# Expert tiles: the tokens' transposes move from TensorE to 32x32 block transposes on VectorE

## The chip, the cores and the metric

The kernel runs on one core of one Trainium2 chip. Times are device microseconds of one execution. The kernel before takes 1641.98 us, the median of 3 runs (1639.44 to 1642.45).

## The reference

Two layers work on x of 4 x 512 tokens with 512 features; each adds an attention part and a feed-forward part to x, and each part reads the layer-normed x. Layer 0 has a score attention against a context and a Hadamard-rotated, quantised feed-forward network. Layer 1 has an attention with 32 heads and then the routed mixture of experts, which is what the change touches:

```python
logits = jnp.einsum('td,de->te', x, gate_w)
top_logits, top_idx = jax.lax.top_k(logits, K)          # K = 2 of E = 8 experts
top_w = jax.nn.softmax(top_logits, axis=-1)
cw = jnp.zeros((T, E)).at[jnp.arange(T)[:, None], top_idx].add(top_w)
for e in range(E):
    h = jax.nn.silu(x @ w0[e]) * (x @ w1[e])            # 512 -> 1024
    out = out + cw[:, e:e + 1] * (h @ wo[e])            # 1024 -> 512
```

T is 2048 tokens, and everything is fp32.

## The kernel before

All stages before the experts keep their code and aren't described here. The last of them sorts the tokens: each token's normed row of 512 values, with its weight for the chosen expert in column 512, is written to `sorted_x` in HBM twice, once for each of its two experts, at a place where the tokens of one expert follow each other. The experts then work on tiles of 128 sorted rows. There are always 39 tiles (`MTILES`), also where the experts have fewer; a small table, `tile_plan`, says for each tile where its rows lie, which expert's weights it takes and where its result goes. Each engine reads its entries of the plan into registers with a load (TENSOR_LOAD in the order of instructions).

The order of the work is written out by hand, one program for each engine, held together by semaphores. `tile_loop` runs the steps 0, 1 and 2, then a hardware loop of two steps a turn, then the last two steps. A step i has these parts:

- ScalarE's DMA queue loads the rows of tile i + 2 (`load`, L1539), 128 rows of 528 values.
- TensorE multiplies tile i by the gate and the up weights (`products`, L2976 to L2978): two halves of 512 inner columns, 24 products each. An fp32 value is kept as two fp32r parts, so that a product of a 128-row chunk is three instructions: first part by first, first by second, second by first.
- TensorE transposes the rows of tile i + 1 into bank 4 of PSUM (`transpose_x`, L2954): four transposes of 128x128.
- TensorE multiplies the inner values of tile i - 1 by the down weights (`down`), 24 products, and then transposes the inner values of tile i (L2999), 8 transposes.
- ScalarE takes the Silu of each half (L1555), copies the transposed tokens as their first part (`x_first`, L1547) and the transposed inner values as theirs (L1560), and issues the store of the result (`store`, L1543).
- VectorE multiplies Silu and up (L2236), makes the second parts (`x_second`, L2256, and L2246), scales the result by the row weight (`move_y`, L2263) and copies the row weight out of the loaded tile (`row_weight`, L2252).
- GpSimd splits the weights of the coming experts into their parts (L1075, L1076). It starts on an expert's down weights when the last down block of the expert before is done. SP loads the weights.

Semaphores that the text speaks of: `e_ld` (a tile's rows are loaded), `e_xtr` (transposed), `e_xh` and `e_xl` (first and second part made), `e_gu` (a half of gate and up is done), `e_xw` (row weight), `e_y` (result scaled), `e_hl` (second part of the inner values). Ahead of the first tile TensorE runs `unread` products (L2860), whose results nobody reads, and waits for the sorted rows; VectorE works out the places of the results (`result_slots`, L2272 to L2279).

## Time and profile before

| | us |
|---|---|
| median of 3 runs | 1641.98 |
| profiled execution | 1643.14 |
| its span | 1641.3 |
| TensorE busy in the span | 1565.4 (95%) |
| VectorE busy | 938.9 (57%) |
| ScalarE busy | 717.1 (44%) |
| GpSimd busy | 702.1 (43%) |
| mean granted TensorE clock | 0.985 of full |
| first expert product | 928.31 into the span |

The expert loop is the stretch from 928 us to the end. In the rows below, PE is TensorE, DVE VectorE, ACT ScalarE, POOL GpSimd; SPq and ACTq are DMA issues of SP and ScalarE. A row in order of time has the start (us from the span's start), the duration (us), engine, line and operation, output <- inputs, the shape, and in brackets the idle time of the engine ahead of it and what ended it. Matmuls overlap: two starts tell more than one duration. "issue" is time in which an engine waited for nothing that the profile shows. A row of the busy time by stretches has the stretch, its length, then the busy time (and number of instructions) of PE, the weight loads of PE, DVE, ACT and POOL, the granted clock of TensorE as a share of 2.4 GHz, the DMA engines' busy share and GB/s. A row of a line's instructions has their count, the least, median and greatest duration in ns, and the first and last start. A row of the page's costliest groups has the busy time and mean ns after the first bar, and the idle time before with what ended it after the second.

### The profile page before, as it was taken

The page shows a single profiled execution, that of the slowest core. Times are in us where ns is not written, and L with a number is a line of the kernel's source. Part 1 is how long each engine was busy: PE and PEld are TensorE (multiplying, and loading weights), DVE is VectorE, ACT ScalarE, POOL GpSimd, SP SyncE. Part 2 cuts the span into 40 slices and gives each one's busy share as a digit, 9 for nine tenths or more (in the row PEclk, how much of TensorE's full clock was granted, in tenths as well). Part 3 has the DMA queues.
Part 4 walks back from the last instruction along what each step waited for, and adds up shares of the span by engine and source line. Part 5 has one row for each costly group of instructions (what it writes and reads, how often), then busy time and mean ns, then how long its engine had stood idle before and what let it go on. Part 6 is the DMA issues. An engine that isn't in the chain of part 4 may idle for free.

```text
span 1641.3 us, 24692 instructions
## 1 busy us (share of the span) xinstructions
PE 1565.4 (95%) x8277; PEld 1046.3 (64%) x8278; DVE 938.9 (57%) x1540; ACT 717.1 (44%) x1166; POOL 702.1 (43%) x479
## 2 busy tenths in 40 slices
PE   6879999999999999999998799999999999999998
PEld 4565757575753333434333788888888888888886
DVE  6898979797888898988884622222222222222221
ACT  5885646464537777777676211111111111111111
POOL 2224352534513125353464756651781270930074
PEclk9889999999999999999999999999999999999999
DMA  9189800000331445353431642323421323510088
GB/s 355 51 306 386 323 1 1 1 1 1 101 80 49 134 125 155 91 146 102 146 104 61 211 155 95 132 77 137 179 77 34 133 77 128 180 39 26 32 142 211
DMA packets 90945, 196.18 MB, mean 120 GB/s; under 512 B 7153, under 2 KB 9074, under 8 KB 90226
## 3 DMA queue, kind: packets, MB, share of 16 engines
q1 hardware_dynamic: 71746, 156.68, 28.5%
q0 software_dynamic: 7168, 17.04, 4.6%
q10 hardware_dynamic: 11952, 21.43, 3.9%
q8 instruction: 46, 0.75, 0.2%
q14 instruction: 33, 0.27, 0.1%
HBM read 113.28 MB, written 81.32 MB: 119 GB/s over the span
## 4 chain that ended last, share of the span: by engine, by line
PE 78%; DVE 13%; ACT 3%; issue 3%; POOL 2%; DMA 1%; another core or an unknown queue 0%; SPq 0%; DVEq 0%; POOLq 0%; ACTq 0%
PE psum L2976 13%; PE psum L2978 13%; PE psum L2977 13%; PE psum L2619 7%; PE psum L2830 6%; PE psum L2819 5%; PE psum L2634 5%; DVE neg_max L2094 4%; PE psum L2793 3%; PE psum L2664 3%; PE psum L2999 2%; DMA x_tiles<-in_x 1%; PE psum L2954 1%; DVE ternary_rows L1697 1%; PE psum L2809 1%
## 5 line engine op out<-in xcount | busy, mean ns | idle before, releaser
L2094 DVE TENSOR_REDUCE neg_max<-psum 128x2 f32<-128x1024 f32 x248 | 291.9, 1220 | 44.1 <-PE psum L2793 42.0
L1450 ACT ACTIVATE probabilities<-psum 128x512 f32<-128x512 f32 x512 | 270.3, 603 | 82.2 <-PE psum L2819 78.1
L2236 DVE TENSOR_TENSOR expert_inner<-psum,expert_inner 128x512 f32<-128x512 f32 x78 | 53.9, 692 | 382.6 <-ACT expert_inner L1555 377.5
L2976 PE MATMUL psum<-expert_weight_parts,sorted_tokens_t_first 128*128 x624 | 249.7, 400 | 4.9 <-issue 3.1
L2978 PE MATMUL psum<-expert_weight_parts,sorted_tokens_t_second 128*128 x624 | 246.3, 395 | 0.0
L2977 PE MATMUL psum<-expert_weight_parts,sorted_tokens_t_first 128*128 x624 | 246.2, 395 | 0.0
L1555 ACT ACTIVATE expert_inner<-psum 128x512 f32<-128x512 f32 x78 | 46.7, 599 | 390.2 <-PE psum L2978 390.2
L2819 PE MATMUL psum<-query_rows,key_rows 50*128 50x512 f32 x512 | 181.4, 445 | 5.1 <-ACT probabilities L1450 1.7
L2793 PE MATMUL psum<-key_rows,query_rows 48*128 48x512 f32 x496 | 173.0, 480 | 6.0 <-DVE neg_max L2094 3.3
L2830 PE MATMUL psum<-probabilities,value_and_one 128*32 128x512 f32 x1024 | 139.8, 619 | 1.5 <-ACT probabilities L1450 0.9
L2976 PEld LDWEIGHTS psum<-expert_weight_parts,sorted_tokens_t_first 128*128 128x128 f32 x624 | 117.3, 188 | 32.4 <-issue 5.9
L2819 PEld LDWEIGHTS psum<-query_rows,key_rows 50*128 50x128 f32 x512 | 78.3, 187 | 90.0 <-issue 37.7
L2978 PEld LDWEIGHTS psum<-expert_weight_parts,sorted_tokens_t_second 128*128 128x128 f32 x624 | 117.4, 188 | 27.3
L2977 PEld LDWEIGHTS psum<-expert_weight_parts,sorted_tokens_t_first 128*128 128x128 f32 x624 | 117.4, 188 | 26.2
L1075 POOL CAST expert_weight_parts<-wo_of_expert 128x2048 fp32r<-128x2048 f32 x16 | 30.4, 1897 | 241.5 <-PE psum L2978 241.5
L1560 ACT ACTIVATE expert_inner_t_first<-psum 128x512 fp32r<-128x512 f32 x78 | 42.6, 596 | 202.0 <-PE psum L2999 202.0
L2976 PE MATMUL psum<-expert_weight_parts,expert_inner_t_first 128*128 128x512 f32 x312 | 125.9, 403 | 1.6 <-DVE expert_inner_t_second L2246 1.6
L2978 PE MATMUL psum<-expert_weight_parts,expert_inner_t_second 128*128 128x512 f32 x312 | 122.2, 392 | 0.0
L2977 PE MATMUL psum<-expert_weight_parts,expert_inner_t_first 128*128 128x512 f32 x312 | 122.1, 391 | 0.0
L2263 DVE TENSOR_SCALAR expert_out<-psum,row_weight 128x512 f32<-128x512 f32 x39 | 29.3, 750 | 161.0 <-PE psum L2978 156.9
L866 POOL TENSOR_TENSOR inner_half_rotated_t<-inner_t 128x512 f32<-128x512 f32 x56 | 75.4, 1367 | 80.0 <-DVE inner_t L1935 79.7
L1028 POOL TENSOR_TENSOR x_tiles<-x_tiles,attended_normed 128x256 f32<-128x256 f32 x31 | 22.7, 733 | 202.2 <-DVE attended_normed L2141 202.2
(317 smaller groups left out, 2966.0 us busy)
## 6 DMA issues: line engine op xcount, KB each, us to landing
sorted_x<-zero_rows SPq DMA_DIRECT2D x9, 3960.0 KB, 30.5
w_of_odd_expert<-in_L_ffn_w SPq DMA_DIRECT2D x8, 2048.0 KB
wo_of_expert<-in_L_ffn_wo SPq DMA_DIRECT2D x7, 2048.0 KB, 8.5
query_rows<-query_rows_of_units SPq DMA_DIRECT2D x64, 192.0 KB, 3.5
w_of_even_expert<-in_L_ffn_w SPq DMA_DIRECT2D x6, 2048.0 KB, 10.7
sorted_tokens<-sorted_x ACTq DMA_DIRECT2D x39, 264.0 KB, 2.7
sorted_y<-expert_out ACTq DMA_DIRECT2D x39, 256.0 KB, 2.1
query_rows_of_units<-dims_first SPq DMA_DIRECT2D x32, 256.0 KB
```

Of the source, the lines that this page charges most:

```text
L866: nc.gpsimd.tensor_tensor(Z[:, chunk_of(r, h) * SEQ:(chunk_of(r, h) + 1) * SEQ], y[0], y[1], op).then_inc(b_half, 1)
L1450: nc.scalar.activation(prob[t % 2][:, i * SEQ:(i + 1) * SEQ], ring(("score", n)), ACT.Exp, scale=HD ** -0.5).then_inc(c_e, 1)
L2094: nc.vector.tensor_reduce(of_pair[:, p, st, :], ring(("max", (m, i))).rearrange("p (h n) -> p h n", h=2), AX.X, ALU.max, negate=True).then ...
L2236: nc.vector.tensor_tensor(h, bank[2 * half + 1], h, ALU.mult).then_inc(e_h, 1)
L2619: last = nc.tensor.matmul(bank[4 + 2 * w + h], wgu_t[w][:, k * FF + f * P:k * FF + (f + 1) * P], q_t[:, k * SEQ:(k + 1) * SEQ], start=(k = ...
L2634: last = nc.tensor.matmul(bank[4 + g], y[:, at:at + P], had[:, k * D:(k + 1) * D], start=(k + part == 0), stop=(k + part == DC))
L2793: done = nc.tensor.matmul(ring(job)[:, h * SEQ:(h + 1) * SEQ], q_r[m % 4][rows, p * SEQ + st * P:p * SEQ + (st + 1) * P], k_r[m % 4][rows, ...
L2819: nc.tensor.matmul(ring(("score", n)), k_r[u % 4][rows, t * P:(t + 1) * P], q_r[u % 4][rows, p * SEQ:(p + 1) * SEQ], start=True, stop=True ...
L2830: last = nc.tensor.matmul(bank[7][32 * h:32 * h + 32, :], v_u[u % KVH][:, t * 32:(t + 1) * 32], prob[t % 2][:, h * SEQ:(h + 1) * SEQ], sta ...
L2976: nc.tensor.matmul(out_bank, hi[:, cols], w_r[:, bass.ds(w_at, 512)], start=start, stop=False)
L2977: nc.tensor.matmul(out_bank, hi[:, cols], w_r[:, bass.ds(w_at + BLOCK, 512)], start=False, stop=False)
L2978: return nc.tensor.matmul(out_bank, lo[:, cols], w_r[:, bass.ds(w_at, 512)], start=False, stop=stop)
```

## The change

TensorE's four token transposes go. In their place VectorE transposes the tile as 32x32 blocks in one instruction (`x_transposed`), from SBUF into bank 4, between the two halves' products of the step. A block transpose alone doesn't bring features across groups of 32 partitions, so the load does: tile i is loaded by four DMAs (`load`, a = 0 to 3), each of which places the 128 features a*128 to a*128 + 127 of all 128 rows on 32 partitions. The features then stand in bank 4 in another order, and the host lays out the rows of `w0` and `w1` in that order (`laid_out`), outside the kernel. The row weight is no longer part of the tile; it has its own load of 16 columns, straight into `row_w` (`load_row_weight`), behind the store of a step. The inner values are transposed on TensorE as before.

```diff
-        x_in = [small.tile(f"sorted_tokens{i}", [P, WIDE]) for i in range(2)]
+        x_in = [small.tile(f"sorted_tokens{i}", [P, D]) for i in range(2)]
...
-        row_w = [small.tile(f"row_weight{i}", [P, 1]) for i in range(2)]
+        row_w = [small.tile(f"row_weight{i}", [P, WIDE - D]) for i in range(2)]
...
-            sp.wait_ge(e_ld[1], 16)
+            sp.wait_ge(e_ld[1], 64)
...
                 def load(i, parity):
-                    act.wait_ge(e_xtr, i + 1)
                     if not (static(i) and i < 2):
-                        act.wait_ge(e_xw, i - 1)
-                    nc.scalar.dma_start(x_in[parity][:], sorted_x[bass.ds(row_of(i), P), :]).then_inc(e_ld[parity], 16)
+                        act.wait_ge(e_xtr, i - 1)
+                    rows = sorted_x[bass.ds(row_of(i), P), 0:D]
+                    for a in range(4):
+                        nc.scalar.dma_start(x_in[parity][32 * a:32 * a + 32].rearrange("r (b c) -> r b c", c=P),
+                                            rows[:, a * P:(a + 1) * P].rearrange("(b r) c -> r b c", r=32)).then_inc(e_ld[parity], 16)
+
+                def load_row_weight(i, parity):
+                    if not static(i) or i > 0:
+                        act.wait_ge(e_xw, 16 * i)
+                    if not static(i) or i > 1:
+                        act.wait_ge(e_y, i)
+                    nc.scalar.dma_start(row_w[parity][:], sorted_x[bass.ds(row_of(i), P), D:WIDE]).then_inc(e_xw, 16)
...
                 def x_first(i):
-                    act.wait_ge(e_xtr, 2 + i + 1)
+                    act.wait_ge(e_xtr, i + 1)
+                    act.wait_ge(e_gu, 1 + 2 * i)
...
                         store(i - 1, 1 - parity)
+                    load_row_weight(i, parity)
...
                         nc.vector.tensor_tensor(h, bank[2 * half + 1], h, ALU.mult).then_inc(e_h, 1)
+                        if half == 0 and (not static(i) or i + 1 < MTILES):
+                            x_transposed(i + 1, 1 - parity)
...
-                    if not static(i) or i + 1 < MTILES:
-                        row_weight(i + 1, 1 - parity)
...
-                def row_weight(i, parity):
-                    if not (static(i) and i < 2):
-                        dve.wait_ge(e_y, i)
-                    dve.wait_ge(e_ld[parity], 8 * (i - parity) + 16)
-                    nc.vector.tensor_copy(row_w[parity][:], x_in[parity][:, D:D + 1]).then_inc(e_xw, 1)
+                def x_transposed(i, parity):
+                    if not static(i) or i > 0:
+                        dve.wait_ge(e_xl, i)
+                    dve.wait_ge(e_ld[parity], 32 * (i - parity) + 64)
+                    nc.vector.transpose(bank[4].rearrange("p (k b r) -> p b k r", k=4, b=4),
+                                        x_in[parity][:].rearrange("p (b k j) -> p b k j", b=4, k=4)).then_inc(e_xtr, 1)
...
                     dve.wait_ge(e_wo, i + 2)
+                    dve.wait_ge(e_xw, 16 * i + 16)
...
+                x_transposed(0, 0)
                 x_second(0)
-                row_weight(0, 0)
...
-                def transpose_x(i, parity):
-
-                    pe.wait_ge(e_ld[parity], 8 * (i - parity) + 16)
-                    for k in range(DC):
-                        last = nc.tensor.transpose(bank[4][:, k * P:(k + 1) * P], x_in[parity][:, k * P:(k + 1) * P], ident[:])
-                    last.then_inc(e_xtr, 1)
-
...
-                    if not static(i) or i + 1 < MTILES:
-                        transpose_x(i + 1, 1 - parity)
...
-                transpose_x(0, 0)
...
-            pe.sem_inc(e_xtr, 2)
...
+def laid_out(name, a):
+
+
+    if name not in ("L1_ffn_w0", "L1_ffn_w1"):
+        return a
+    experts, rows, columns = a.shape
+    a = a.reshape(experts, 4, 4, 32, columns).swapaxes(1, 2)
+    return np.ascontiguousarray(a.reshape(experts, rows, columns))
```

TensorE's order in the second step of a loop turn, from the last gate/up products to the first down product, before:

```order
L2977 MATMUL psum<-expert_weight_parts,sorted_tokens_t_first 128x512
L2978 MATMUL psum<-expert_weight_parts,sorted_tokens_t_second 128x512
L2954 MATMUL psum<-ident,sorted_tokens_261 128x128 [waits e_ld1]
L2954 MATMUL psum<-ident,sorted_tokens_261 128x128 x3
L2971 TENSOR_LOAD tile_plan
L2971 ISA x2
L2976 MATMUL psum<-expert_weight_parts,expert_inner_t_first 128x512 [waits wo_parts,e_y,e_hl]
```

And of the changed kernel, whose lines L2977 and L2982 to L2984 are the ones that were L2971 and L2976 to L2978:

```order
L2983 MATMUL psum<-expert_weight_parts,sorted_tokens_t_first 128x512
L2984 MATMUL psum<-expert_weight_parts,sorted_tokens_t_second 128x512
L2977 TENSOR_LOAD tile_plan
L2977 ISA x2
L2982 MATMUL psum<-expert_weight_parts,expert_inner_t_first 128x512 [waits wo_parts,e_y,e_hl]
```

The four transposes and their wait for the load are gone, and the load of the plan stands right behind the last gate/up product.

VectorE's order in the first step of a loop turn, before (the steps' two products are the first and third row):

```order
L2236 TENSOR_TENSOR expert_inner<-psum,expert_inner 128x512 [waits e_silu]
L2234 REGISTER_ALU
L2236 TENSOR_TENSOR expert_inner<-psum,expert_inner 128x512 [waits e_silu]
L2255 REGISTER_ALU
L2256 TENSOR_TENSOR sorted_tokens_t_second<-psum,sorted_tokens_t_first 128x512 [waits e_xh]
L2259 REGISTER_ALU
L2262 REGISTER_ALU [waits e_wo]
L2263 TENSOR_SCALAR expert_out_266<-psum,row_weight_264 128x512 [waits e_st0]
L2251 ISA [waits e_y]
L2252 COPY row_weight_264<-sorted_tokens_260 128x1 [waits e_ld0]
L2246 TENSOR_TENSOR expert_inner_t_second<-psum,expert_inner_t_first 128x512 [waits e_hh] x2
```

And of the changed kernel:

```order
L2247 TENSOR_TENSOR expert_inner<-psum,expert_inner 128x512 [waits e_silu]
L2261 REGISTER_ALU
L2262 ISA [waits e_xl]
L2263 STREAM_TRANSPOSE psum<-sorted_tokens_260 128x4x4x32 [waits e_ld0]
L2245 REGISTER_ALU
L2247 TENSOR_TENSOR expert_inner<-psum,expert_inner 128x512 [waits e_silu]
L2267 REGISTER_ALU
L2268 TENSOR_TENSOR sorted_tokens_t_second<-psum,sorted_tokens_t_first 128x512 [waits e_xh]
L2272 ISA [waits e_wo]
L2275 REGISTER_ALU [waits e_xw]
L2276 TENSOR_SCALAR expert_out_266<-psum,row_weight_264 128x512 [waits e_st0]
L2257 TENSOR_TENSOR expert_inner_t_second<-psum,expert_inner_t_first 128x512 [waits e_hh] x2
```

The block transpose stands between the two products, and the copy of the row weight is gone.

ScalarE's order at the start of the expert loop, the loads of tiles 0 and 1 and the first part of tile 0, before:

```order
L1529 TENSOR_LOAD tile_plan [waits d_sc_odd,e_xtr,d_sc_even,d_plan]
L1529 ISA x2
L1539 ISA
L1539 DMA sorted_tokens_260<-sorted_x 128x528
L1529 TENSOR_LOAD tile_plan [waits e_xtr]
L1529 ISA x2
L1539 ISA
L1539 DMA sorted_tokens_261<-sorted_x 128x528
L1547 ACTIVATE sorted_tokens_t_first<-psum 128x512 [waits e_xtr]
```

And of the changed kernel, tile 0 and the first load of tile 1:

```order
L1529 TENSOR_LOAD tile_plan [waits d_sc_odd,d_sc_even,d_plan]
L1529 ISA x2
L1540 ISA
L1540 DMA sorted_tokens_260<-sorted_x 32x4x128
L1540 ISA
L1540 DMA sorted_tokens_260<-sorted_x 32x4x128
L1540 ISA
L1540 DMA sorted_tokens_260<-sorted_x 32x4x128
L1540 ISA
L1540 DMA sorted_tokens_260<-sorted_x 32x4x128
L1529 TENSOR_LOAD tile_plan
L1529 ISA x2
```

Each tile has four loads where it had one; the copy of tile 0's first part now stands behind eight.

## Rows read from the trace of the kernel before

**Rows 1.** TensorE's loop by the busy time by stretches.

```profile
1200.00:1400.00 200.00, 200.00 (x934) 164.17 (x933) 45.49 (x77) 30.87 (x56) 79.77 (x26) 1.00 0.27 93
```

**Rows 2.** VectorE in order of time, one tile.

```profile
1207.70 0.69 DVE L2236 TENSOR_TENSOR expert_inner<-psum,expert_inner 128x512 f32<-128x512 f32 x1 [4.80 <-ACT expert_inner L1555]
```

**Rows 3.** ScalarE and its DMA queue in order of time, the tile behind.

```profile
1214.66 0.36 ACTq L1543 DMA_DIRECT2D sorted_y<-expert_out  x1
1215.87 0.35 ACTq L1539 DMA_DIRECT2D sorted_tokens<-sorted_x  x1
1219.55 0.60 ACT L1555 ACTIVATE expert_inner<-psum 128x512 f32<-128x512 f32 x1 [5.02 <-PE psum L2978]
```

**Rows 4.** All engines in order of time, the start of the expert loop.

```profile
922.00 4.13 PE L2860 MATMUL psum<-ident 128*128 128x128 f32 x20 [3.00 <-DMA sorted_x<-rows_of_batch,slot]
922.68 4.15 DVE L2279 TENSOR_TENSOR slot_of_result<-slot_f,slot_moved_by 128x16 int32<-128x16 f32 x1
923.01 1.45 ACTq L1539 DMA_DIRECT2D sorted_tokens<-sorted_x  x2
925.97 0.60 PE L2954 MATMUL psum<-ident,sorted_tokens 128*128 128x128 f32 x4
926.60 0.60 ACT L1547 ACTIVATE sorted_tokens_t_first<-psum 128x512 fp32r<-128x512 f32 x1 [17.10 <-PE psum L2954]
926.75 1.89 POOL L1075 CAST expert_weight_parts<-wo_of_expert 128x2048 fp32r<-128x2048 f32 x1
927.23 0.69 DVE L2256 TENSOR_TENSOR sorted_tokens_t_second<-psum,sorted_tokens_t_first 128x512 fp32r<-128x512 f32 x1 [0.40 <-ACT sorted_tokens_t_first L1547]
928.31 0.49 PE L2976 MATMUL psum<-expert_weight_parts,sorted_tokens_t_first 128*128 x1 [1.75 <-DVE sorted_tokens_t_second L2256]
```

**Rows 5.** TensorE in order of time, the tile of rows 2.

```profile
1206.64 0.40 PE L2978 MATMUL psum<-expert_weight_parts,sorted_tokens_t_second 128*128 x1
1206.87 0.60 PE L2954 MATMUL psum<-ident,sorted_tokens 128*128 128x128 f32 x4
1207.22 0.47 PE L2976 MATMUL psum<-expert_weight_parts,expert_inner_t_first 128*128 128x512 f32 x1
1207.54 0.39 PE L2977 MATMUL psum<-expert_weight_parts,expert_inner_t_first 128*128 128x512 f32 x1
...
1212.57 0.40 PE L2978 MATMUL psum<-expert_weight_parts,expert_inner_t_second 128*128 128x512 f32 x1
```

**Rows 6.** TensorE in order of time, the last tile.

```profile
1623.22 0.39 PE L2978 MATMUL psum<-expert_weight_parts,sorted_tokens_t_second 128*128 x1
1623.45 0.39 PE L2976 MATMUL psum<-expert_weight_parts,expert_inner_t_first 128*128 128x512 f32 x1
...
1628.72 0.40 PE L2978 MATMUL psum<-expert_weight_parts,expert_inner_t_second 128*128 128x512 f32 x1
```

**Rows 7.** The instructions of line L2954.

```profile
L2954 PE MATMUL psum<-ident,sorted_tokens x156: 270/272/273, 926.0 to 1603.9; 128*128 128x128 f32 x156
```

**Rows 8.** The page's costliest groups, VectorE's reduction.

```profile
L2094 DVE TENSOR_REDUCE neg_max<-psum 128x2 f32<-128x1024 f32 x248 | 291.9, 1220 | 44.1 <-PE psum L2793 42.0
```

**Rows 9.** The instructions of line L1539, and the landing of its loads.

```profile
L1539 ACTq DMA_DIRECT2D sorted_tokens<-sorted_x x39: 344/351/357, 923.0 to 1576.7; - x39
...
DMA to landing us min/median/max: 2.5/2.7/5.9
```

**Rows 10.** GpSimd and TensorE in order of time, an expert switch.

```profile
1005.74 4.61 POOL L1076 TENSOR_TENSOR expert_weight_parts<-wo_of_expert,expert_weight_parts 128x2048 fp32r<-128x2048 f32 x1 [0.18 <-POOL expert_weight_parts L1075]
...
1008.99 0.48 PE L2976 MATMUL psum<-expert_weight_parts,expert_inner_t_first 128*128 128x512 f32 x1
```

**Rows 11.** The busy time by stretches, around the loop's start.

```profile
922.00:926.00 4.00, 4.00 (x21) 4.00 (x22) 3.93 (x4) 0.00 (x0) 3.81 (x2) 0.57 0.37 81
926.00:930.00 4.00, 2.25 (x13) 1.77 (x11) 1.59 (x3) 1.13 (x2) 3.82 (x3) 1.00 0.51 129
```

**Rows 12.** TensorE in order of time, behind tile 0.

```profile
943.36 0.49 PE L2976 MATMUL psum<-expert_weight_parts,sorted_tokens_t_first 128*128 x1 [1.52 <-issue]
```

2 lines of the change are left out of this document (1 added, 1 removed).

## The prediction

> **What bounds the kernel now.** I read the busy time by stretch first, then TensorE's rows in order of time within one expert tile, then the waits. In the expert loop TensorE never rests: it is busy 200.00 of 200.00 us at full granted clock [rows 1]. One tile is a gate/up block of 48 products, the four token transposes of L2954, a down block of 24 products and eight inner transposes of L2999. VectorE and ScalarE wait for TensorE each time: the second half's product on VectorE starts after 4.80 us of idling [rows 2], the first Silu of a tile after 5.02 us [rows 3]. So what leaves TensorE's queue inside this loop comes off the end, and what arrives on the other queues is free as long as it fits in those idle times. Two places are different: the start of the loop, where TensorE waits for the token tile itself [rows 4], and tile 0, where it waits for VectorE after the transposes.
>
> **What the four transposes cost.** The last gate/up product starts at 1206.64, the transposes at 1206.87, the first down product at 1207.22 and the second at 1207.54 [rows 5]. Without transposes each start would follow the last by some 0.23 us: 0.35 us for the transposes, and 0.32 instead of 0.23 for the first product behind them, together 0.44. The trace has a counterpart: the last tile has no token transposes, and its down block follows the gate/up block directly. From the last gate/up start to the last down start it takes 1628.72 - 1623.22 = 5.50 us [rows 6], against 1212.57 - 1206.64 = 5.93 with them [rows 5]: 0.43. I take 0.44, of a tile of 18.1 us (the last gate/up products at 1206.64 and 1623.22 are 23 tiles apart). There are 156 transposes, four a tile, for 39 tiles [rows 7]. Those of tile 0 are in the start (below). Those of tile 1 run in step 0, in which TensorE next waits for VectorE's product for the inner transposes, so that they hide there and their going saves nothing. That leaves 37 tiles: 37 x 0.44 = 16.3 us.
>
> **Is the down block ready at once?** The rows of the order show that a TENSOR_LOAD of the plan stands between the gate/up block and the down block, and that the transposes gave TensorE work over it. In the last tile the same load stands there without transposes, and the products go on after 0.23 us [rows 6]. So I cost this at zero. If the cover is gone after all, the price is the first rival's.
>
> **VectorE: one block transpose a tile.** The trace shows no such instruction. It moves 512 fp32 columns on 128 partitions from SBUF to PSUM. The nearest row is the product at 0.69 us for 512 columns [rows 2]; from above, the reduction takes 1.22 us for 1024 columns [rows 8], which I use as the upper bound as if the transpose took twice as long a column. I take 0.7 and keep 0.5 to 1.22; below 0.5 nothing in the rows reaches for 512 columns. It stands between the two products, where VectorE idles 4.80 us [rows 2], so even 1.22 is hidden. Queued behind it is the second product, which would be late only if the transpose took longer than that idling. Its wait for the previous tile's second part is over half a tile earlier, and its wait for the four loads over a whole tile earlier. The 0.15 us copy of the row weight goes, off the path.
>
> The Trainium skill bears on this place ("VectorE: DVE Perf Modes", section "The three transpose paths"): it gives VectorE 311 ns for a 128x128 bf16 tile and advises TensorE for full 128x128 transposes. By that figure four such pieces would be an estimated 1.24 us, against 0.7 by the rows; in the loop both are hidden, and at the start it would add 0.5 us to the sum. Against its advice speaks that TensorE is the engine that is full here.
>
> **ScalarE's queue.** It issued one store and one load a tile; now it issues one store, four token loads and one row weight load. A load costs 0.35 us of issue [rows 9], with the address set ahead of it some 0.4 us. Four more are 1.6 us, and the row weight's has a plan load of its own: the store and the load that follow each other with one such load between are 1.2 us apart in start [rows 3], so 1.2 us more. All of this stands after the last copy of a tile and ahead of the next Silu. Today the load starts at 1215.87 and is over at 1216.22, the Silu begins at 1219.55 [rows 3]; moved back by 1.2 and lengthened by 1.2 (three more token loads) it is over at 1218.6 even where its own earlier start isn't counted, against a Silu now due 0.44 earlier, at 1219.1. Even if each issue took twice as long (+2 us), the first half's Silu would be 1.5 us late; its product is wanted only after the down block, some 11 us on, and the second Silu, too, waits about 5 us today. Nothing there reaches TensorE. The copy of the token's first part on ScalarE keeps its place behind the second Silu, and the second part on VectorE too. The loads are issued a tile and more ahead of their use, with a landing of 2.7 us, at most 5.9 [rows 9]. SP's second load for the odd expert waits for four loads in place of one: some 2 us later, on weights not used before tile 3.
>
> **The expert switches.** GpSimd splits the down weights of the next expert after the last down block of the one before. The second half is ready at 1005.74 + 4.61 = 1010.35, while the down block that wants it starts at 1008.99 and reaches it 12 products on, at 1008.99 + 0.32 + 11 x 0.229 = 1011.8 [rows 5, 10]. That is 1.5 us of slack; a faster TensorE takes 0.44 of it. No new wait.
>
> **The start.** Today: loads issued from 923.01, landed and transposed on TensorE at 925.97, first part from 926.60, second from 927.23, first product at 928.31 [rows 4]. Now the fourth piece of tile 0 is issued 3 x 0.4 us later, at 924.2, and lands by 2.7 us at 926.9; VectorE is busy with L2279 until 922.68 + 4.15 = 926.83 [rows 4], so that these two bounds coincide. Block transpose 926.95 to 927.65, first part (0.60) to 928.3, second (0.69) to 929.0, first product 0.4 us behind, as today: 929.45, so 1.15 us later. Bounds: 0.9 if the pieces land as early as the one load did, and 4.5 if the fourth takes 5.9 us.
>
> On top comes the clock. TensorE's last warming product ends at 926.13 [rows 4]; today the token transposes carry it on to 926.57 and it idles 1.74 us, with granted clock 1.00 from 926 to 930 [rows 11]. Now it idles 3.3 us. After the idle 3.00 us up to 922.00 [rows 4] the granted clock was 0.57 over 922 to 926, that is mostly the lower level, 1.2 GHz [rows 11]: 4 x 0.43 = 1.7 us of work lost. I expect the same for the first products of tile 0: 1.7 us. The start costs 1.15 + 1.7 = 2.85 us.
>
> The long L2279 is itself worth a look: 4.15 us for 16 columns, ending with GpSimd's instruction beside it. If the block transpose were held up in this way too, it could wait as long as a GpSimd instruction, 4.61 us [rows 10]. In the loop that is still within the idling of 4.80 us but for the transpose's own length, and the second product would be 0.5 us late with some 4 us to spare; at the start it would cost 1.7 us more (GpSimd's next instruction begins at 926.75 and takes 1.89 [rows 4]).
>
> The Trainium skill ("SBUF — State Buffer", section "SBUF: two separate sides") says that VectorE and GpSimd exclude each other on a shared port pair where the VectorE instruction has two SBUF inputs or runs in a two-port mode. L2279 has two SBUF inputs, so the trace agrees (4.15 us). A transpose with one SBUF input and a PSUM output is neither by this rule, and the sum stays as it is.
>
> **Sum.** -16.3 + 2.85 = -13.45 us. The profiled execution took 1643.14 us, 1.84 more than its span, and that part doesn't change; it becomes 1629.7. It lies 1.16 us above the median of the three runs, 1641.98, so for the median I predict 1628.5.
>
> **Rivals.** (1) Slower than before: the plan load between gate/up and down block is exposed. Inside the loop, products with register addresses take more instructions each than those of the down block, and TensorE's sequencer may not be far enough ahead once the transposes don't give it time. After tile 0, where the sequencer had been held by a wait, three plan loads cost 1.52 us before the first product [rows 12], so one is 0.51: 37 x 0.51 = 18.9, and the time is 1628.5 + 18.9 = 1647.4. It decides from a gap of 13.45 / 37 = 0.36 us a tile on, above which the change loses. Against it: rows 6, which have this load without a gap, at the same place behind the same products. Chance 0.05; a smaller gap of 0.1 to 0.3 us a tile (1632 to 1639.6) gets 0.08. (2) The clock stays up at the start, as after 1.74 us: 1628.5 - 1.7 = 1626.8. For it: there are only two idle times to go by, 1.74 and 3.00 us. Against it: 3.3 us is longer than the one that brought the clock down. 0.22. (3) The start is much longer, by a late fourth piece, by the hold-up of the transpose, or both: 1.7 to 3.4 us more, 1630.2 to 1631.9. 0.12. (4) The queue of ScalarE or a weight split becomes the bound of some tiles and eats most of the gain: 1638 to 1643. What speaks against it is the slack above. 0.03. The forecast itself (within 1.3 us of 1628.5) has 0.50.
>
> "Same" is within 0.2%, 3.3 us, about what a measurement of this kernel can tell from none. Faster: 0.50 + 0.22 + 0.12 and most of the small gap, 0.90; same: the rest of it and (4), 0.05; slower: rival (1), 0.05. The range runs from 1625 (clock up, 0.47 in place of 0.44 a tile: 1625.7) to 1635 (a gap of 0.15 a tile: 1634; or a long start).
>
> **What would show it.** The period from one tile's gate/up block to the next falls by 0.44 us; the last gate/up start and the first down start are 0.23 us apart; the rows of the block transpose last 0.7 us and stand between the two products; the first expert product starts near 929.5 and the granted clock over the 4 us behind it is near 0.57; no wait of TensorE for VectorE or GpSimd appears within the loop. A gap behind each gate/up block, a product on VectorE that comes after the down block's end, or a TensorE wait on weights would make the prediction wrong.

## The result, and the profile after

The kernel after takes 1625.88 us, the median of 4 runs (1625.21 to 1627.64), beside 1642.22 for the kernel before (4 runs, 1639.44 to 1648.2). The ratio is 0.9895, 95% interval 0.9874 to 0.9916: 17.2 us less, 13.8 to 20.7. In a later comparison (e16 below) it was 0.9884 (0.9870 to 0.9898), 19.0 us less. I had forecast 13.5 us less. The sign was right and the size too small: a term was missing. Taken off the 1641.98 us that the prediction starts from, the ratio gives 1624.7 us, just below the low end of its range, 1625.

The profiled execution took 1626.53 us, with a span of 1624.6. By starts of instructions of both traces:

| stretch | before | after | difference |
|---|---|---|---|
| span's start to the first token load | 923.01 | 926.67 | +3.66 |
| to the first expert product | 5.30 | 6.16 | +0.86 |
| first to last gate/up product of tile 0 | 11.06 | 13.08 | +2.02 |
| last gate/up product of tile 0 to that of tile 1 | 15.04 | 14.71 | -0.33 |
| last gate/up product of tile 1 to that of tile 38 | 668.80 | 645.68 | -23.12 |
| last gate/up product of tile 38 to the end | 18.11 | 18.25 | +0.14 |

The first line isn't the change's: the code up to there is the same. In twenty traces of kernels with the same code there, the first load lay between 917.5 and 926.7 us. This trace has the latest, with a granted clock of 0.92 from 800 us to 926, against 0.99 from 800 us to 917 in one of the earliest (e5). That part varies from run to run, and medians average over it. What needs an explanation is -23.12: 37 tiles shorter by 0.625 us each, where I had said 0.44.

TensorE in order of time in the kernel after, from the last gate/up product of one tile to the last down product (start, duration, engine, line and operation, operands):

```profile
1257.11 0.40 PE L2984 MATMUL psum<-expert_weight_parts,sorted_tokens_t_second 128*128 x1
1257.34 0.40 PE L2982 MATMUL psum<-expert_weight_parts,expert_inner_t_first 128*128 128x512 f32 x1
1257.58 0.40 PE L2983 MATMUL psum<-expert_weight_parts,expert_inner_t_first 128*128 128x512 f32 x1
...
1262.69 0.39 PE L2984 MATMUL psum<-expert_weight_parts,expert_inner_t_second 128*128 128x512 f32 x1
```

The down block follows the gate/up block at 0.23 us, the plan load between them is fully covered, and there is no slow first product (0.24, against 0.32 in [rows 5]). But from last gate/up start to last down start it takes 5.58 us, not the 5.50 of [rows 6]: the down products now follow each other at (1262.69 - 1257.58) / 22 = 0.2323 us, against (1212.57 - 1207.54) / 22 = 0.2286 in [rows 5]. The gate/up block went the other way. Its 13th and its last product, first in the kernel before and then in the kernel after:

```profile
1252.56 0.40 PE L2976 MATMUL psum<-expert_weight_parts,sorted_tokens_t_first 128*128 x1
1260.69 0.39 PE L2978 MATMUL psum<-expert_weight_parts,sorted_tokens_t_second 128*128 x1
```

```profile
1249.17 0.39 PE L2982 MATMUL psum<-expert_weight_parts,sorted_tokens_t_first 128*128 x1
...
1257.11 0.40 PE L2984 MATMUL psum<-expert_weight_parts,sorted_tokens_t_second 128*128 x1
```

35 products take 8.13 us before and 7.94 after, 0.2323 and 0.2269 each. Over all tiles of the loop the pitch of gate/up products (time from start to start) is 0.2328 before and 0.2267 after, that of down products 0.2289 and 0.2329. Both traces have a granted clock of 1.00 and a full TensorE here, the after's as [rows 1] was:

```profile
1200.00:1400.00 200.00, 199.98 (x917) 164.97 (x917) 53.80 (x81) 32.17 (x58) 85.80 (x28) 1.00 0.28 93
```

The same products on the same engine at the same clock have another pitch. A tile's -0.625 us is made up so, mean over the loop: gap for the transposes -0.355, first down product -0.09, gate/up block -0.24, down pitch +0.085, the rest -0.02. The first two are my 0.44; the next two I did not have.

VectorE and ScalarE in the loop, where [rows 2, 3] stood:

```profile
1229.91 0.39 ACTq L1552 DMA_DIRECT2D sorted_y<-expert_out  x1
1231.31 0.37 ACTq L1548 DMA_DIRECT2D row_weight<-sorted_x  x1
1232.89 1.89 ACTq L1540 DMA_DIRECT2D sorted_tokens<-sorted_x  x4
...
1234.99 0.60 ACT L1565 ACTIVATE expert_inner<-psum 128x512 f32<-128x512 f32 x1 [5.27 <-PE psum L2984]
```

```profile
1235.62 0.69 DVE L2247 TENSOR_TENSOR expert_inner<-psum,expert_inner 128x512 f32<-128x512 f32 x1 [5.06 <-ACT expert_inner L1565]
1236.23 0.72 DVE L2263 STREAM_TRANSPOSE psum<-sorted_tokens 128x512 f32<-128x512 f32 x1
```

Five loads now stand in ScalarE's queue, the last over at 1234.78; the Silu at 1234.99 still waits for TensorE, as does VectorE's product. The block transpose takes 0.72 us, directly behind the first half's product. The start, where [rows 4] stood:

```profile
925.18 3.74 PE L2873 MATMUL psum<-ident 128*128 128x128 f32 x32 [0.94 <-issue]
926.42 4.12 DVE L2292 TENSOR_TENSOR slot_of_result<-slot_f,slot_moved_by 128x16 int32<-128x16 f32 x1
926.67 4.59 ACTq L1540 DMA_DIRECT2D sorted_tokens<-sorted_x  x8
930.47 0.71 DVE L2263 STREAM_TRANSPOSE psum<-sorted_tokens 128x512 f32<-128x512 f32 x1
931.37 0.60 ACT L1557 ACTIVATE sorted_tokens_t_first<-psum 128x512 fp32r<-128x512 f32 x1 [18.07 <-DVE psum L2263]
932.00 0.69 DVE L2268 TENSOR_TENSOR sorted_tokens_t_second<-psum,sorted_tokens_t_first 128x512 fp32r<-128x512 f32 x1 [0.82 <-ACT sorted_tokens_t_first L1557]
932.83 0.79 PE L2982 MATMUL psum<-expert_weight_parts,sorted_tokens_t_first 128*128 x1 [3.91 <-DVE sorted_tokens_t_second L2268]
```

The transpose begins as L2292 ends (930.47); ScalarE, whose eight load issues end at 931.26, takes its copy up at 931.37. TensorE idles 3.91 us, and the granted clock over 931 to 935 is 0.50, the lower level, where [rows 11] had 1.00:

```profile
931.00:935.00 4.00, 2.17 (x5) 1.79 (x6) 0.87 (x2) 1.68 (x2) 3.82 (x2) 0.50 0.58 112
```

### The profile page after: what moved, and what is told of

It reads as the page before. It is cut to its first block, busy times and chain, and to the rows that moved or that the text cites. A ratio compares the mean times of both kernels' runs of the same rounds, so it can differ in the third digit from the quotient of the medians.

```text
span 1624.6 us, 25055 instructions
## 1 busy us (share of the span) xinstructions
PE 1550.1 (95%) x8121; PEld 1036.4 (64%) x8122; DVE 959.1 (59%) x1540; ACT 716.6 (44%) x1166; POOL 701.9 (43%) x479
## 4 chain that ended last, share of the span: by engine, by line
PE 78%; DVE 13%; ACT 3%; issue 3%; POOL 2%; DMA 1%; ACTq 0%; SPq 0%; DVEq 0%; POOLq 0%; another core or an unknown queue 0%
PE psum L2982 13%; PE psum L2984 13%; PE psum L2983 13%; PE psum L2632 7%; PE psum L2843 6%; PE psum L2832 6%; PE psum L2647 5%; DVE neg_max L2105 4%; PE psum L2806 3%; PE psum L2677 3%; PE psum L3003 2%; DMA x_tiles<-in_x 1%; PE psum L2593 1%; PE psum L2822 1%; DVE ternary_rows L1708 1%
## 5 line engine op out<-in xcount | busy, mean ns | idle before, releaser
L2982 PE MATMUL psum<-expert_weight_parts,sorted_tokens_t_first 128*128 x624 | 248.0, 397 | 5.6 <-DVE sorted_tokens_t_second L2268 3.9
L2984 PE MATMUL psum<-expert_weight_parts,sorted_tokens_t_second 128*128 x624 | 244.3, 392 | 0.0
L2832 PE MATMUL psum<-query_rows,key_rows 50*128 50x512 f32 x512 | 185.8, 456 | 5.7 <-ACT probabilities L1450 1.6
L2806 PE MATMUL psum<-key_rows,query_rows 48*128 48x512 f32 x496 | 178.5, 490 | 5.1 <-DVE neg_max L2105 2.5
L2982 PEld LDWEIGHTS psum<-expert_weight_parts,sorted_tokens_t_first 128*128 128x128 f32 x624 | 117.7, 189 | 31.1 <-issue 7.2
L2984 PEld LDWEIGHTS psum<-expert_weight_parts,sorted_tokens_t_second 128*128 128x128 f32 x624 | 117.7, 189 | 24.6
L2982 PE MATMUL psum<-expert_weight_parts,expert_inner_t_first 128*128 128x512 f32 x312 | 123.6, 396 | 1.6 <-DVE expert_inner_t_second L2257 1.6
L2984 PE MATMUL psum<-expert_weight_parts,expert_inner_t_second 128*128 128x512 f32 x312 | 123.0, 394 | 0.0
```

The source lines that it names most:

```text
L2806: done = nc.tensor.matmul(ring(job)[:, h * SEQ:(h + 1) * SEQ], q_r[m % 4][rows, p * SEQ + st * P:p * SEQ + (st + 1) * P], k_r[m % 4][rows, ...
L2832: nc.tensor.matmul(ring(("score", n)), k_r[u % 4][rows, t * P:(t + 1) * P], q_r[u % 4][rows, p * SEQ:(p + 1) * SEQ], start=True, stop=True ...
L2982: nc.tensor.matmul(out_bank, hi[:, cols], w_r[:, bass.ds(w_at, 512)], start=start, stop=False)
L2984: return nc.tensor.matmul(out_bank, lo[:, cols], w_r[:, bass.ds(w_at, 512)], start=False, stop=stop)
```

## The experiments

The suspicion came from the diff: `x_in` shrinks from 2112 to 2048 bytes a buffer and `row_w` grows from 32 to 64, so that all buffers laid out behind them move. The tokens' parts (in a gate/up product the stationary operand, the 128x128 one whose weight load comes ahead of it) move down by 128 bytes, the inner values' parts (the stationary operand of down) by 64. Below, the **offset** of a part is its byte address less that of the expert weights (the moving operand, of 512 columns), modulo 256, as the kernel lays them out. Before: tokens' parts 128, inner parts 192. After: 0 and 128. Theory A: the pitch follows these places. Theory B: it follows the instruction stream, from which transposes have gone. Pitches are means over the loop, from the 13th product of each block on; "loop" is the stretch of 37 tiles.

**e1, the kernel before without the token transposes of tiles 1 to 38** (every tile then works on tile 0's tokens):

```diff
...
-                    if not static(i) or i + 1 < MTILES:
-                        transpose_x(i + 1, 1 - parity)
```

(The waits for the transposes go with them.)

> The kernel before with TensorE's token transposes of tiles 1 to 38 left out (tile 0 keeps its own): every tile works on tile 0's tokens, so the part of the computation left out is the transposes of the others. All tiles in SBUF stay where they were; one load a tile, the row weight's copy and everything else stay. It asks whether the going of the transposes alone makes the gate/up products denser (in the changed kernel their pitch is 0.2268 us from the tenth on, against 0.2328 before). Theory A (places: it is the new SBUF places of the tokens' parts, 128 bytes lower, that make gate/up products denser and the down products slower): pitch stays at 0.233 in gate/up and 0.229 in down; 0.44 a tile saved, 37 tiles, 16.3 us and nothing lost at the start: 1626. Theory B (instruction stream: without the transposes TensorE's queue is fed otherwise): gate/up pitch 0.227, 0.62 a tile or more, 23 us: 1619.

1627.26 us (1626.48 to 1633.21), ratio 0.9896 (0.9876 to 0.9916); pitches 0.2325 and 0.2293, loop 654.71. The transposes are worth 14.1 us in the loop, and the pitches stay within 0.0004 us of those of before.

**e2, the kernel after with both parts at the addresses of before:**

```diff
-        x_in = [small.tile(f"sorted_tokens{i}", [P, D]) for i in range(2)]
+        x_in = [small.tile(f"sorted_tokens{i}", [P, WIDE])[:, 0:D] for i in range(2)]
...
-        row_w = [small.tile(f"row_weight{i}", [P, WIDE - D]) for i in range(2)]
+        small.at += 64
...
+        row_w = [small.tile(f"row_weight{i}", [P, WIDE - D]) for i in range(2)]
```

> The changed kernel with the tokens' tiles padded to their old width and the row weights put at the end, so that the tokens' parts and the inner values' parts lie at exactly the SBUF places of the kernel before. Theory A (places): the gate/up pitch goes back to 0.233 and the down pitch to 0.229; the gate/up blocks grow by 0.25 us x 38, the down blocks shrink by up to 0.08 x 38: 6 to 9 us slower than the changed kernel, about 1633. Theory B (instruction stream): no difference, 1626.

1628.99 us (1628.48 to 1630.42), ratio 0.9910 (0.9889 to 0.9931); pitches 0.2327 and 0.2288, the values of before; loop 654.76. Its 13th and last gate/up product, 8.14 us apart:

```profile
1245.43 0.39 PE L2983 MATMUL psum<-expert_weight_parts,sorted_tokens_t_first 128*128 x1
1253.57 0.40 PE L2985 MATMUL psum<-expert_weight_parts,sorted_tokens_t_second 128*128 x1
```

**e3, the kernel before with both parts at the addresses of after:**

```diff
-        x_in = [small.tile(f"sorted_tokens{i}", [P, WIDE]) for i in range(2)]
+        hole = Map(nc, small.at, small.at + 2 * 4 * D)
+        small.at = hole.end
...
+        hole2 = Map(nc, small.at, small.at + 2 * 64 + 2 * 4 * D)
+        small.at = hole2.end
+        x_in = [h.tile(f"sorted_tokens{i}", [P, WIDE]) for i, h in enumerate((hole, hole2))]
...
```

> The kernel before with the tokens' parts and the inner values' parts at the SBUF places of the changed kernel (the loaded tiles, results and row weights moved around them); nothing else is changed. Theory A (places): gate/up pitch 0.227, about 9 us faster than before, 1633, less if the down blocks get slower. Theory B (instruction stream): as before, 1642.

1635.6 us (1630.6 to 1638.17), ratio 0.9944 (0.9922 to 0.9966); pitches 0.2266 and 0.2317, loop 660.70. So a kernel that still transposes on TensorE gets the fast gate/up pitch, too:

```profile
1250.61 0.39 PE L2980 MATMUL psum<-expert_weight_parts,sorted_tokens_t_first 128*128 x1
1258.54 0.39 PE L2982 MATMUL psum<-expert_weight_parts,sorted_tokens_t_second 128*128 x1
```

Theory A holds in both directions, and Theory B falls. In e3's trace the clock also fell at the start, and tile 0's gate/up block took 13.52 us in place of 11.06, so the loop, 8.1 us shorter than before, says more here than the time.

**e4, the kernel after with the places of the results worked out behind step 0's start:**

```diff
                 plan_tiles()
-                result_slots()
...
+                result_slots()
```

> The changed kernel with VectorE's working out of the results' places (its last instruction 4.1 us long beside GpSimd's) behind tile 0's block transpose and second part instead of ahead of them. If that instruction is what holds the block transpose of tile 0 (in the changed kernel's trace the transpose starts at 930.47, when it ends, and the fourth load was issued by about 928), the first gate/up product comes 0.5 to 1.5 us earlier against the first token load's issue (6.16 us now), and the time falls by 1 us, or by 2.7 if the clock then stays up. If the loads' landing is what holds it: no change, 1626.

1629.15 us (1626.68 to 1630.31), ratio 0.9906 (0.9884 to 0.9929). The transpose began 3.49 us after the first load issue, then held by the landing, in place of 3.80; the first product came after 6.16 us all the same, since ScalarE's eight issues held its copy. And the moved work now held up tile 0's product on VectorE: tile 1 began 9.06 us after tile 0's last gate/up product in place of 3.95. A miss as an improvement, but it gives the three bounds of the start.

```profile
923.49 0.73 DVE L2262 STREAM_TRANSPOSE psum<-sorted_tokens 128x512 f32<-128x512 f32 x1 [7.54 <-DMA sorted_tokens<-sorted_x]
924.70 0.60 ACT L1557 ACTIVATE sorted_tokens_t_first<-psum 128x512 fp32r<-128x512 f32 x1 [18.18 <-DVE psum L2262]
...
925.94 4.47 DVE L2285 TENSOR_TENSOR region_moved<-experts_end,experts_tiles 128x8 f32<-128x8 f32 x1
930.45 1.80 DVE L2286 SCALAR_TENSOR_TENSOR region_moved<-region_moved,expert_regions 128x8 f32<-128x8 f32 x1
```

**e5, the kernel after with the inner parts at offset 0:**

```diff
+        small.at += 128
         h_d = small.tile("expert_inner", [P, MOE])
```

> The kernel after, with the two transposed parts of the inner rows 128 bytes further up in SBUF (from a byte address that is 0 modulo 256 to one that is 128 modulo 256, where the tokens' parts and all expert weights lie in the kernel after). Theory A (the pitch of products follows the places of stationary and moving operand against each other, 128 apart slow, 64 or 192 apart middling, equal fast): the down block's pitch falls from 0.233 to 0.2267 us, 24 products x 38 x 0.0062 = 5.7 us, so 1625.9 - 5.7 = 1620.2 us; the gate/up pitch stays 0.2267. Theory B (the pitch has to do with the block's own code, or with what other engines do beside it): down pitch stays at 0.233, time 1625.9 us.

1618.5 us (1614.62 to 1623.19), ratio 0.9858 (0.9830 to 0.9886); both pitches 0.2267, loop 642.51. Its second and last down product are 4.99 us apart, 22 x 0.2268. The inner parts lie at 256 modulo 512 here and the tokens' parts at 0, with one pitch, so that the offset is taken modulo 256 (e9 has it the other way round):

```profile
1264.31 0.39 PE L2984 MATMUL psum<-expert_weight_parts,expert_inner_t_first 128*128 128x512 f32 x1
...
1269.30 0.39 PE L2985 MATMUL psum<-expert_weight_parts,expert_inner_t_second 128*128 128x512 f32 x1
```

**e6, the kernel after with everything 64 bytes up:**

```diff
-        first = (nc.sbuf_base + 63) // 64 * 64
+        first = (nc.sbuf_base + 63) // 64 * 64 + 64
```

> The kernel after, with every buffer in SBUF 64 bytes further up, so that all distances between buffers stay: tokens' parts at 192 modulo 256, inner parts at 64, expert weights at 192. Theory A1 (what counts is the distance between stationary and moving operand modulo 256): pitches as in the kernel after, 0.2267 gate/up and 0.233 down, time 1625.9 us. Theory A2 (what counts is the stationary operand's own address modulo 256, with 0 slow, 64 middling, 128 fast): the down block falls to 0.229, and gate/up goes to an unknown value for 192, 0.229 if it is like 64: +48 x 38 x 0.0023 - 24 x 38 x 0.0041 = +4.2 - 3.7, time 1626.4 us, told from A1 by the pitches and not by the time.

1624.43 us (1623.11 to 1628.23), ratio 0.9882 (0.9858 to 0.9905); pitches 0.2267 and 0.2329 as in the kernel after. What counts is the offset, not the stationary operand's own address.

**e7, the kernel after with 20 more unread products:**

```diff
                 pe.wait_ge(*scattered(BATCH - 1))
-                unread(10)
+                unread(30)
```

> The kernel after, with 30 in place of 10 unread 128x128 products behind the last scatter. They take 0.12 us each at this point, so TensorE is busy 2.3 us longer and idle 1.6 us instead of 3.9 before the first expert product. If the fallen clock there comes from that idle time: granted clock 1.00 in the 4 us behind the first product, the first gate/up block 11.0 us instead of 13.08, time 1625.9 - 2.0 = 1623.9 us, start of the first product unchanged. If the clock falls for another reason (work of the attention phases before it): block stays at 13.1 us, time 1625.9 us.

1622.11 us (1619.16 to 1623.93), ratio 0.9870 (0.9844 to 0.9897), 2.3 us under e6, which has the pitches of the kernel after; the two intervals overlap. TensorE idled 0.27 us before the first expert product, the clock stayed at 1.00, and the first block took 10.76 us:

```profile
929.00:933.00 4.00, 3.73 (x19) 3.04 (x19) 0.00 (x0) 1.28 (x1) 4.00 (x2) 1.00 0.88 234
```

Twenty were too many: the operands were there at 928.04, the first product began at 929.82. From the first load issue to the end of tile 0's gate/up block it took 18.56 us, against 18.53 in e6 and 19.24 in the kernel after: what the clock gave back went into the late start. So the 2.3 us under e6 aren't the clock's; the loop, where e7 has no edit, took 643.77 us against 648.09.

**e8, inner parts at offset 0, 30 unread products, ScalarE's first copy ahead of the second tile's loads:**

```diff
                 load(0, 0)
-                load(1, 1)
                 x_first(0)
+                load(1, 1)
```

> The kernel after, with the inner parts 128 bytes up, the 20 more unread products, and ScalarE's first x_first ahead of the second tile's loads. Theory A with a start bound by ScalarE's eight load issues: down pitch 0.2267 (-5.7 us), first block at full clock (-2.0), and x_first up to 0.5 us earlier (the block transpose ends 0.4 us before the issues do), in all -8.1 us: 1617.8 us. Theory B for the places: 1625.9 - 2.4 = 1623.5 us.

1613.16 us (1610.61 to 1617.83), ratio 0.9820 (0.9790 to 0.9850), 4.6 us under the expected; 3 of them lie in the loop (639.55 against 642.51 in e5), where e8 has no edit of its own, so nothing is read from them (2.6 of the 3 are in the gap ahead of the gate/up blocks, see below). The copy began 4.53 us after the first load issue in place of 4.70, and the second part was ready after 5.85 in place of 6.02; the first product again waited for the unread ones.

**e9, the kernel before with both parts at offset 0:**

```diff
+        small.at += 128
         x_hi = small.tile("sorted_tokens_t_first", [P, D], F32R)
...
+        small.at += 192
         h_d = small.tile("expert_inner", [P, MOE])
```

> The kernel before, with the tokens' parts 128 bytes further up and the inner parts 320 bytes, so that both, like the expert weights, lie at 128 modulo 256. Theory A (only the distance of a stationary part from the weights modulo 256 counts): gate/up pitch 0.2267 in place of 0.2328 us, block 11.025 to 10.77, down pitch 0.2267 in place of 0.2289: about -0.255 and -0.06 us a tile, x 38 = -12 us, so 1642.9 - 12 = 1631 us. With this the change itself, at good places on both sides, is worth 1631 less the 1618.5 us of the kernel after with its inner parts 128 bytes up, about 12.5 us. Theory B (the pitch goes with something else in the kernel after): 1643 us, pitches as before.

1631.24 us (1628.77 to 1632.68), ratio 0.9933 (0.9915 to 0.9952); both pitches 0.2267, loop 658.56. As expected: two added lines of layout are worth 11 us without the change. Against e5 the change itself is worth 16.05 us in the loop.

**e10, the kernel after with both parts 64 bytes up** (offsets 64 and 192):

```diff
+        small.at += 64
         x_hi = small.tile("sorted_tokens_t_first", [P, D], F32R)
```

> The kernel after, with tokens' parts and inner parts 64 bytes further up: tokens' parts 64 above the weights modulo 256, inner parts 64 below. Theory A1 (distance 0 gives 0.2267, 128 gives 0.233, 64 on either side 0.229): gate/up pitch 0.229, down pitch 0.229; +48 x 38 x 0.0023 - 24 x 38 x 0.004 = +4.2 - 3.6, time 1626.5 us. If only the very same place modulo 256 is fast and any other costs the same, gate/up goes to 0.233 and the time to about 1637 us.

1633.67 us (1629.85 to 1638.16), ratio 0.9949 (0.9930 to 0.9967); pitches 0.2334 and 0.2320. My middling value for 64 was wrong: 64 above is as slow as 128. And the inner parts, at the very address of the kernel before, were slower than there (0.2289).

**e11, e8 with 20 unread products:**

```diff
-                unread(30)
+                unread(20)
```

> The kernel e8 (inner parts 128 bytes up, first ScalarE product ahead of the second tile's loads) with 20 unread products in place of 30. In e8 the unread products ended 1.9 us after the operands of the first expert product were there; with ten fewer, at 0.143 us each, it starts 1.4 us earlier, and TensorE is idle for none or for under 1 us before it, so the clock stays: 1613.2 - 1.4 = 1611.8 us. If the clock falls all the same, the first block takes 2.0 us longer and the time is 1613.8 us.

1612.42 us (1611.35 to 1618.47), ratio 0.9826 (0.9806 to 0.9846), with the clock at full (first block 10.76 us). Against e8 (0.9820, in another comparison) no difference can be told by the times. By the traces the start is 1.9 us shorter: from the first load issue to the end of tile 0's gate/up block 16.76 us, against 18.69 in e8 and 16.37 in the kernel before.

**e12 to e15** go after e10's two surprises, one run each. e12: inner parts alone 64 bytes up (offsets 0 and 192). e13: tokens' parts at 192, inner parts at 0. e14: tokens' parts at 32, inner parts at 0. e15: e10 again. The edit is e10's with other numbers, here e14's:

```diff
+        small.at += 32
         x_hi = small.tile("sorted_tokens_t_first", [P, D], F32R)
...
+        small.at += 96
         h_d = small.tile("expert_inner", [P, MOE])
```

> The kernel after, with the inner parts alone 64 bytes up (64 below the weights modulo 256, the very address that they have in the kernel before and in e10). In the kernel before the down pitch at this address is 0.2289 us, in e10 it is 0.2320. Theory P (the places of the two operands alone set the pitch): 0.2289 or 0.2320, and e10 run again gives the same as this one; time 1625.9 - 3.7 or - 0.9. Theory Q (something else beside the operands counts, such as where the buffers lie that are written meanwhile): this kernel and e10 differ. Gate/up pitch 0.2267 by both.

> The kernel after, with the tokens' parts at 64 below the weights modulo 256 and the inner parts at the weights' own place. If distance -64 is cheaper than +64: gate/up pitch 0.2289 us, block 10.88 us. If every distance but 0 is slow: 0.2328 to 0.2334, block 11.06 us. Down pitch 0.2267 by both. Time 1618.5 + 3.9 = 1622 us, or 1618.5 + 10.5 = 1629 us.

> The kernel after, with the tokens' parts at 32 above the weights modulo 256 and the inner parts at the weights' own place. If any distance but 0 is slow: gate/up pitch 0.2328 to 0.2334 us and the time 1629 us. If the pitch grows with the distance: between 0.2267 and 0.2334, and the time 1619 to 1629 us. Down pitch 0.2267 by both.

> The kernel e10 again, on another occasion and beside e12. If pitches are a property of the kernel: gate/up 0.2334 and down 0.2320 us again. If they belong to the chip or the day: other values, the down pitch 0.2289 as in the kernel before.

| | time | offset of tokens' parts, gate/up pitch | offset of inner parts, down pitch |
|---|---|---|---|
| e12 | 1620.0 | 0, 0.2267 | 192, 0.2291 |
| e13 | 1619.67 | 192, 0.2289 | 0, 0.2266 |
| e14 | 1630.45 | 32, 0.2334 | 0, 0.2267 |
| e15 | 1634.12 | 64, 0.2334 | 192, 0.2315 |

With all the others: offset 0 gives 0.2266 to 0.2267 (every time, either block; tile 1 of e4, whose block began at a granted clock of 0.50, is left out), 192 gives 0.2288 to 0.2293 (six traces), 128 gives 0.2317 to 0.2330, and 32 and 64 give 0.2334. The exception is the down block of e10, which e15 repeats: with the tokens' parts at 64, inner parts at 192 cost 0.2315 to 0.2320. So the operands' offset isn't all, and by their own pitches e12 and e15 side by side show that it is a property of the kernel. What else counts there stays open. e14's slow gate/up pitch, 35 products in 8.17 us:

```profile
1246.59 0.40 PE L2984 MATMUL psum<-expert_weight_parts,sorted_tokens_t_first 128*128 x1
1254.76 0.40 PE L2986 MATMUL psum<-expert_weight_parts,sorted_tokens_t_second 128*128 x1
```

**e16 to e18** size the shares, on one chip, four to six runs each: the kernel after, e2 and e5 again.

> The kernel after as it is, beside e17 and e18 on one chip, to size the share of the places. Pitches 0.2267 (gate/up) and 0.233 us (down). If the whole surplus over the forecast is the places, it is 48 x 38 x 0.0061 - 24 x 38 x 0.0041 = 7.4 us faster than e17; if the times of the first batch are right as they are, 2.5 to 3.5 us.

> The kernel e2 again (the change, with both parts at the addresses of the kernel before). Pitches 0.2328 and 0.2289 us. By my forecast of the change alone 13.5 us faster than the kernel before; e2 had a ratio of 0.991, 14.8 us.

> The kernel e5 again (both parts at the weights' place modulo 256). Pitches 0.2267 us in both blocks: 5.7 us faster than e16, 13.1 us faster than e17.

| | median | ratio, 95% | loop | pitches |
|---|---|---|---|---|
| before | 1640.65 | | | |
| e17, change at the old places | 1629.61 | 0.9930 (0.9916 to 0.9944) | 653.81 | 0.2327, 0.2289 |
| e16, kernel after | 1622.85 | 0.9884 (0.9870 to 0.9898) | 647.05 | 0.2266, 0.2328 |
| e18, both at offset 0 | 1617.12 | 0.9852 (0.9838 to 0.9867) | 643.62 | 0.2267, 0.2267 |

By the medians the new places are worth 6.8 us (7.4 expected), the better ones another 5.7 (5.7 expected), and the change without them 11.0 us. By the ratios, which the first section goes by, it is 7.5, 5.3 and 11.5 us (9.2 to 13.8).

## Why the prediction was wrong

**The step that failed** is the sum's silent assumption in "What the four transposes cost": that a tile loses 0.44 us and its 72 products stay as they are. The pitches did not stay: gate/up went from 0.2328 to 0.2267 us, down from 0.2289 to 0.2329. The sum lacks a term for the places, 48 x 38 x 0.0061 - 24 x 38 x 0.0040 = 7.5 us by the pitches, 6.8 by the medians of e16 and e17. With it the forecast of -13.5 would have been about -20, more than the -17.2 measured and near the -19.0 of e16, for the term of the transposes was 1.3 us too large (below): -15.0 - 6.8 + 2.9 = -18.9. The two errors have opposite signs, and so the time missed by less than the places alone would have made it. With the places held at the old ones the measured gain is 11.5 us (e17) and 14.8 (e2), both by their ratios, on both sides of the 13.5. The time alone would have misled: 1625.88 us lies within 1 us of rival 2's 1626.8, whose clock did not come.

It could have been suspected from the rows: the kernel before has the same kind of product at two pitches, 0.2323 in gate/up and 0.2286 in down, both at a granted clock of 1.00. I used 0.23 for both and asked no more. And the diff changes the size of two buffers ahead of the operands.

**The transposes, 0.44 us a tile.** Right in kind, a little too large. Their gap (0.355) and the slow product behind them (0.09) went in every kernel that had none. But the loop gave back 14.0, 15.0, 14.9 or 16.0 us (before to e2 and e17, e9 to e18 and e5), 15.0 on average in place of 16.3. The rest is between the first inner transpose and the next gate/up block: this time has a median of 0.81 to 0.84 us in all of them, but a mean of 0.87 and 0.89 in the two kernels with transposes and 0.92 to 0.94 in the four without. Ahead of the even tiles 4 to 34 its mean is 0.79 us in all six; ahead of the odd ones, the first of a turn of the hardware loop, it is 0.83 and 0.85 with transposes and 0.97 to 1.00 without. The longest, up to 2.6 us, stands ahead of the last tile with or without them. The trace names nothing that TensorE waits for there. Without the transposes alone (e1) the odd tiles have 0.83, and with 20 more unread products at the start (e7) 0.80, against 0.91 in the kernel after, so why it comes and goes isn't settled.

**The plan load behind gate/up.** Right: 1257.11 to 1257.34, and in all 37 tiles of the loop at most 0.23 us. Rival 1 is out.

**The block transpose.** 0.72 us where I took 0.7; the price estimated from the Trainium skill's figure ("VectorE: DVE Perf Modes", section "The three transpose paths"), 1.24 us, was too high. It stood behind the first half's product, nobody waited for it in the loop, and in the loop's rows GpSimd did not hold it up: least, median and greatest duration of all 39 were 714, 717 and 718 ns, and 19 of them ran beside a GpSimd instruction.

```profile
L2263 DVE STREAM_TRANSPOSE psum<-sorted_tokens x39: 714/717/718, 930.5 to 1585.1; 128x512 f32<-128x512 f32 x39
```

The Trainium skill's rule on the shared port ("SBUF — State Buffer", section "SBUF: two separate sides") agrees here, and in e4, where L2285 and L2286, each with two SBUF inputs and 8 columns, took 4.47 and 1.80 us beside GpSimd.

**ScalarE's queue.** Right: the five loads fit. The slack was small, from 1234.78 to 1234.99, where I had worked out 0.5 us.

**The start, +1.15 us for the operands.** Measured +0.86. The two bounds that I had put side by side were real (landing 3.49 us after the first issue, VectorE free after 3.80), but I had missed a third: the second tile's four loads and its plan load stand ahead of ScalarE's copy. In a row one issue follows another after 0.49 us, not 0.4, and all eight with the plan load take 4.59. It took part in deciding: the copy began 0.2 us behind the transpose's end. What made the start come out shorter all the same is the last step: the first product followed the second part's end (932.69) after 0.14 us, where I had carried over the 0.4 of [rows 4]. The lower bound of 0.9 was a slip: with VectorE free at 926.83 it should have been about 1.0.

**The clock, +1.7 us.** Right: idle 3.91 us, granted clock 0.50, first block 2.02 us longer. With TensorE kept busy the clock stays and the block takes 10.76 (e7), so it is the idling that brings it down. Rival 2 is out. How long an idling is enough can't be read from it alone: in e3, whose 1.77 us were no longer than the 1.75 of [rows 4], the clock fell too (first product 0.79 us long, block 13.52). What e3 had besides is another idle time of 1.39 us just ahead of its 0.63 us of token transposes; in [rows 4] the unread products run on into the transposes. The start in all was +2.88 us, the forecast +2.85: the closeness is luck, 0.29 less for the operands and 0.32 more for the clock. In e16's trace the block lost 2.58 us.

**Expert switches, SP's later load, other waits.** No wait of TensorE for another engine within the loop, as forecast. SP's load for the odd expert was issued 6.17 us after the first token load (932.84), in place of 4.33: 1.8 us later where I had said 2, and nothing in the loop waited for it. In step 0 the inner transposes wait 0.97 us for VectorE's product, where they waited 0.54 before: the time of tile 1's token transposes, which hid there, as forecast. The longest wait for another engine behind the start is ahead of the last down block, 1.57 us, the same as in the kernel before:

```profile
PE psum L2982 <- DVE expert_inner_t_second L2257: 1.6, 1, 1.6
1614.73 0.50 PE L2982 MATMUL psum<-expert_weight_parts,expert_inner_t_first 128*128 128x512 f32 x1 [1.57 <-DVE expert_inner_t_second L2257]
```

**What the sum leaves.** In the loop 23.1 us went and at the start 2.9 came, 20.2 in all, more than the 17.2 of the ratio. The trace of after has 3.66 us more ahead of the loop, and that part varied by 9.2 us between traces of the same code. I take the difference for that; it is argued, not shown. In e16's trace the same stretches give 21.8 and 3.4, 18.3 in all, against 19.0 by its ratio.

## What to carry to other kernels

When a change alters the size of any buffer, look at where all the others land: an operand that moved by 64 or 128 bytes cost or gave as much as half of what the change was made for. Try the stationary operand at the same place modulo 256 bytes as the moving one; here, on one kind of product, that gave 11 us on the kernel before by two lines (e9), and with the change, ScalarE's copy ahead of the second tile's loads and some unread products it made the fastest versions, 1612.4 us (e11) and 1613.2 (e8), 1.8% under the kernel before. Two blocks of the same products with different pitches at full clock are the sign to look for.

## What the runs showed of the hardware that was not expected

- The pitch of a 128x128 by 512-column product of fp32r parts depends on where its stationary part lies in SBUF against its moving one: 0.2267 us at offset 0 modulo 256 bytes, mostly 0.229 at 192, 0.232 to 0.233 at 128, 0.2334 at 32 and 64. Shifting both together changes nothing (e6). Offsets of 0 include both 0 and 256 modulo 512 (e5, e9). The reason, and why e10's down block differs, is open.
- TensorE was at the lower of its two clocks, 1.2 GHz, after 2.98 us (e6, e10) to 4.62 us (e13, e14) of idling and once after 1.77 (e3, with 1.39 us of idling shortly before), and at 2.4 GHz after 0.27 us (e7), 1.56 (e9), 1.74 (e1) and 1.75 us [rows 4, 11].
- VectorE's transpose of 32x32 blocks, 128x512 fp32 from SBUF to PSUM: 0.717 us, the same beside a busy GpSimd (19 of 39).
- DMA issues in a row on ScalarE with their addresses from registers start 0.49 us apart, while the issue itself takes 0.33; eight with a plan load between them took 4.59 us.
